# The second FFN in blocks of seven products, its LoRA added to the weights by an accumulating DMA

## What is computed

```
y  = x W^T + 2 * routed LoRA(x)                 # top 2 of 8 experts
x  = x + series(y) + FFN1(y)                    # six powers of a gate; FFN1 has 1248 hidden columns
z  = x W2^T + b + 2 * LoRA(x) of each sequence  # one of 32 adapters
h1 = z (w1 + 2 B1 A1)^T
h3 = z (w3 + 2 B3 A3)^T                         # FFN2 has 1376 hidden columns
g  = silu(h1) * h3
x  = x + g (w2 + 2 B2 A2)^T
```

## Time and profile before

| what | us |
|---|---|
| median of 3 runs | 448.58 (448.51 to 448.97) |
| the profiled execution itself | 448.42 |
| its span, first to last instruction | 446.7 |
| outside the span | 1.72 |
| PE busy | 441.4 of 446.7 |
| DVE busy | 324.0 |
| ACT busy | 212.2 |
| POOL busy | 29.3 |

### The profile page before, as it was taken

One profiled execution on the slowest core, in us unless ns is written; L12 is line 12 of the kernel. 1 busy time (PEld: TensorE's weight loads), 2 busy tenths in 40 slices (PEclk: granted clock), 3 DMA queues, 4 the chain that ended last, 5 costly groups with the idle time before them and its releaser, 6 DMA issues.

```text
span 446.7 us, 5568 instructions
## 1 busy us (share of the span) xinstructions
PE 441.4 (99%) x2009; PEld 363.5 (81%) x2009; DVE 324.0 (73%) x471; ACT 212.2 (48%) x324; POOL 29.3 (7%) x51
## 2 busy tenths in 40 slices
PE   8999999999999999999989999999999999999997
PEld 6788888888888888888778888888888888888886
DVE  5756699667989688896899248989853568887631
ACT  6364452345757447564565527365541124654300
POOL 1004100000001100005200000000000000000000
PEclk9999999999999999999999999999999999999999
DMA  8406800044574655657340010222201122121022
GB/s 301 132 0 195 201 0 1 12 119 117 117 190 118 147 133 121 145 138 198 109 150 6 18 48 18 70 66 61 74 2 41 57 91 66 48 66 53 1 102 87
DMA packets 20299, 40.44 MB, mean 91 GB/s; under 512 B 2672, under 2 KB 4736, under 8 KB 20272
## 3 DMA queue, kind: packets, MB, share of 16 engines
q1 hardware_dynamic: 16992, 32.51, 22.6%
q0 software_dynamic: 3280, 7.58, 9.7%
HBM read 37.98 MB, written 2.10 MB: 90 GB/s over the span
## 4 chain that ended last, share of the span: by engine, by line
PE 95%; DVE 3%; DMA 1%; ACT 0%; issue 0%; ACTq 0%
PE PS L1697 16%; PE PS L1698 16%; PE PS L1699 16%; PE PS L1562 15%; PE PS L1563 15%; PE PS L1564 15%; PE PS L1874 1%; DVE WU L938 1%; DMA X<-in_x 1%; DVE X L1180 1%; PE PS L1576 0%; PE PS L1922 0%; PE PS L1932 0%; PE PS L1933 0%; DVE S L1249 0%; DVE G L938 0%
## 5 line engine op out<-in xcount | busy, mean ns | idle before, releaser
L1697 PE MATMUL PS<-HT,WU 128*128 128x512 f32 x266 | 103.9, 391 | 1.3 <-DVE T L1123 1.0
L1698 PE MATMUL PS<-HT,WU 128*128 128x512 f32 x266 | 103.6, 389 | 0.0
L1699 PE MATMUL PS<-HT,WU 128*128 128x512 f32 x266 | 103.6, 389 | 0.0
L503 ACT ACTIVATE WU<-raw 128x256 fp32r<-128x256 f32 (+2 forms) x55 | 49.0, 897 | 31.0 <-PE PS L1699 15.1
L1697 PEld LDWEIGHTS PS<-HT,WU 128*128 128x128 f32 x266 | 50.0, 188 | 12.7 <-DVE T L1123 1.4
L938 DVE TENSOR_TENSOR WU<-raw,WU 128x256 fp32r<-128x256 f32 (+2 forms) x56 | 56.5, 1014 | 5.1 <-ACT WU L503 5.0
L1699 PEld LDWEIGHTS PS<-HT,WU 128*128 128x128 f32 x266 | 49.9, 188 | 10.5
L503 ACT ACTIVATE PS<-PS 128x512 f32<-128x512 f32 x46 | 26.8, 582 | 66.0 <-PE PS L1699 59.0
L1698 PEld LDWEIGHTS PS<-HT,WU 128*128 128x128 f32 x266 | 50.0, 188 | 10.0
L938 DVE TENSOR_TENSOR G<-T,G 128x1024 fp32r<-128x1024 f32 (+2 forms) x46 | 43.9, 967 | 12.2 <-ACT G L503 11.6
L503 ACT ACTIVATE G<-T 128x1024 fp32r<-128x1024 f32 (+2 forms) x47 | 39.8, 856 | 22.0 <-DVE T L1054 6.8
(11 more groups left out here) (170 smaller groups left out, 713.1 us busy)
## 6 DMA issues: line engine op xcount, KB each, us to landing
raw<-in_pieces SPq DMA_DIRECT2D x73, 256.0 KB, 3.0
raw<-in_parts SPq DMA_DIRECT2D x14, 512.0 KB, 3.6
raw<-in_parts POOLq DMA_DIRECT2D x14, 384.0 KB, 5.0
X<-in_x SPq DMA_DIRECT2D x8, 256.0 KB, 4.9
raw<-in_pieces SPq DMA_DIRECT2D x14, 128.0 KB, 2.8
out_x<-X SPq DMA_DIRECT2D x7, 256.0 KB, 2.0
su_raw<-in_stk_up POOLq DMA_DIRECT2D x6, 192.0 KB, 2.6
T<-in_lora_b POOLq DMA_DIRECT2D x16, 32.0 KB, 2.5
```

What stands on the lines that cost most here:

```text
L503: return nc.scalar.activation(o, i, ACT.Copy)
L1697: pe.matmul(bank, w[:, 1, cols], hi, start=start and kc == 0, stop=False, skip_group_check=not start)
L1698: pe.matmul(bank, w[:, 0, cols], low, start=False, stop=False, skip_group_check=not start)
L1699: mm = pe.matmul(bank, w[:, 0, cols], hi, start=False, stop=kc == 1, skip_group_check=not start)
```

## The change

The second FFN takes the form of the first. `BLOCKS` gets 13 blocks for it: up blocks for chunks 2 to 10 and four down blocks for chunks 2 to 9. Chunks 0 and 1 stay direct (four half steps of the down product for them in place of 12), and chunk 10 goes down directly at the very end, 3 matmuls for each output. From the third block of it on, the low-rank update goes another way: ScalarE copies it, times 2, from PSUM to a tile `delta` (`delta_hi`), GpSimd issues a DMA that adds `delta` to the raw weights in SBUF (`merge_by_dma`), and GpSimd computes the four weight sums itself (`sums`). `ga_raw` and small tiles move into the space of `delta`, which changes no order. At the end of the first FFN (`last`) VectorE does `add_d` ahead of `tail_lo(1)`, and one LoRA tile moves.

```diff
-LAST = len(BLOCKS) - 1
+
+BLOCKS = ([(0,) + b for b in [("u", 0), ("u", 1), ("u", 2), ("u", 3), ("u", 4), ("d", 0), ("d", 1),
+                              ("u", 5), ("u", 6), ("u", 7), ("u", 8), ("d", 2), ("d", 3), ("u", 9)]]
+          + [(1,) + b for b in [("u", 2), ("u", 3), ("u", 4), ("u", 5), ("u", 6), ("d", 0), ("d", 1),
+                                ("u", 7), ("u", 8), ("u", 9), ("u", 10), ("d", 2), ("d", 3)]])
+F2 = 14
+LAST, END = F2 - 1, len(BLOCKS) - 1
+TAIL = (8, 10)
...
+            def sums(q):
+                n = 3 * (merged_by_dma(q) - 1)
+                pool.wait_ge(merged_in, 16 * merged_by_dma(q))
+                pool.wait_ge(w_ready, max(P_TWO[q - 2], P_PASS + 1) + 1)
+                nc.gpsimd.tensor_tensor(sum_at(q, "S1"), raws(q, "A21"), raws(q, "A22"), ALU.add).then_inc(pool_step, 1)
+                nc.gpsimd.tensor_tensor(sum_at(q, "S3"), raws(q, "A11"), raws(q, "A21"), ALU.add).then_inc(pool_step, 1)
+                pool.wait_ge(pool_step, n + 1)
+                nc.gpsimd.tensor_tensor(sum_at(q, "S2"), sum_at(q, "S1"), raws(q, "A11"), ALU.add).then_inc(pool_step, 1)
+                pool.wait_ge(pool_step, n + 3)
+                nc.gpsimd.tensor_tensor(sum_at(q, "S4"), raws(q, "A12"), sum_at(q, "S2"), ALU.add).then_inc(sums_done, 1)
+
+            def merge_by_dma(q):
+                for p in (P_ONE[q], P_TWO[q]):
+                    pool.wait_ge(raw_in[SLOT[p]], raw_count(p))
+                pool.wait_ge(delta_out, merged_by_dma(q))
+                pool.dma_start(merge_region(q), delta[:], accum_op=ALU.add).then_inc(merged_in, 16)
+
+            for q in range(1, 4):
...
+            for q in range(F2 + 2, END + 1):
...
+                merge_by_dma(q)
+                sums(q)
...
+            def delta_hi(q):
+                n = merged_by_dma(q)
+                if n == 1:
+                    act.wait_ge(lora_ready, HALVES)
+                else:
+                    act.wait_ge(merged_in, 16 * (n - 1))
+                act.wait_ge(merge_done, MERGE["block", q] + 1)
+                nc.scalar.activation(delta[:], PS[:, 6:8, :].rearrange("p b n -> p (b n)"), ACT.Copy,
+                                     scale=SCALING).then_inc(delta_out, 1)
...
+                if q < END:
+                    part1_hi(q + 1, p4_done, q)
+                copy_bc(q)
+                if F2 < q <= END - 2:
+                    delta_hi(q + 2)
                 if odd:
...
                     x_out(q, "b")
...
+                if q == END - 1:
+                    merge_piece(P_END, 6)
+                if q == END:
+                    w_lo(P_END, tail_w(0))
+                    x_out(q, "c")
...
                 x_out(q - 1, "c")
-                s2_lo(1)
-                s2_lo(2)
-                add_b1(q)
+                for k in range(3):
+                    s2_lo(k)
+                add_b(q)
                 s2_lo(3)
                 tail_lo(0)
+                add_d(q)
                 tail_lo(1)
-                add_d1(q)
...
+            def block(q):
+                p6(q)
+                if F2 < q <= END - 2:
+                    merge_block(q + 2)
+                if q == END - 1:
+                    merge_piece(P_END, 10, slice(0, D), 6)
+                p5(q)
+                p2(q)
+                p7(q)
+                if q < END and q != LAST:
+                    p1(q + 1)
+                p3(q)
+                p4(q)
...
+            def merge_down(n, odd):
+
+                for j in range(4):
+                    bank = PB[6 + (1 - j % 2 if odd else j % 2)].rearrange("p (o j n) -> p j o n", o=2, j=2)[:, j // 2]
+                    o = S2_B + n % 2 * 2 * P
+                    mm = pe.matmul(bank, S2[:, chunk(2 + 4 * (n // 2) + j)], S2[:, o:o + 2 * P], start=True, stop=True)
                 mm.then_inc(merge_done, 1)
...
+                    (copied_e, END + 1), c_free(END), a_free(END), b_free(END), (out_ready, 1)]
+            for n, (h, o, cols, bank) in enumerate(OUTPUTS):
+                pe.wait_ge(*free[n])
+                pe.wait_ge(g_ready, G_SPLIT[1, 10, h])
+                product(PB[bank][:, cols], tail_w(0), tail_g(1, 10, h)[:, :, cols], chunk(o), True, True).then_inc(down2_done, 1)
```

More of the change, by code:

```diff
@@ L99 @@
 SLOT += [0, 1, 4, 5, 3, 2, 0, 1, 4, 5, 3]
[L100 to L110, removed]
+P_CLASSIC = len(SLOT)
+SLOT += [0, 1, 3, 2]
+for _q in range(F2, len(BLOCKS)):
+    if _q == F2 + 2:
+        P_PASS = len(SLOT)
+        SLOT += [4, 5]
+    P_ONE[_q], P_TWO[_q] = len(SLOT), len(SLOT) + 1
+    SLOT += ((0, 1), (3, 2))[_q % 2]
+P_END = len(SLOT)
+SLOT.append(3)
 PIECES = len(SLOT)
@@ L1479, in _ @@
             su_lo(2)
[L1480 to L1483 removed]
+            sums(F2 + 1)
+            part1_lo(F2 + 1)
+            add_b(F2)
+            add_d(F2)
             g_lo(1)
[L1485 to L1495 removed]
@@ L1553, in _ @@
+            add_b(F2 + 1)
+            add_d(F2 + 1)
+            for j in range(2):
+                w_lo(P_PASS + j, DW[:, j])
+            mul1(1, 3)
+            mul0(1, 3)
+            part1_lo(F2 + 2)
+            pass_add(0)
+            part2_lo(F2 + 2)
+            su_lo(3)
+            pass_add(1)
+            for q in range(F2 + 2, END + 1):
+                steady(q)
             for n, (h, c, cols, bank) in enumerate(OUTPUTS):
+                q = END - 1 if c < 2 else END
+                first = c % 2 == q % 2
+                dve.wait_ge(((out_c, out_a), (out_d, out_b))[h][first], outputs(q))
@@ L1908, in _ @@
+            p6(0)
+            p2(0)
+            p7(0)
+            p1(1)
+            p3(0)
+            p4(0)
+            for q in range(1, F2):
+                block(q)
             for h in range(HALVES):
-                for j in range(C1 - TAIL):
+                for j in range(C1 - TAIL[0]):
                     tail(h, j)
@@ new lines, in _ @@
+            p1(F2 + 1)
+            p3(F2)
+            p4(F2)
+            p6(F2 + 1)
+            for j in range(2):
+                merge_piece(P_PASS + j, j, slice(0, D), 6 + j)
+            p5(F2 + 1)
+            p2(F2 + 1)
+            p7(F2 + 1)
+            p3(F2 + 1)
+            p4(F2 + 1)
+            last = unit(1, 3) + 1
+            ready = [[(copied_e, F2 + 2), (silu[0], last - 1), (silu[1], last - 1), (g_mul[0], last)],
+                     [(pass_added, 1), (silu[0], last), (silu[1], last), (pass_added, 4)]]
@@ new lines, in _ @@
+            for n in range(4):
+                if n == 1:
+                    merge_block(F2 + 3)
+                if n == 3:
+                    p1(F2 + 2)
+                half_step(n, ready[n // 2])
+            for q in range(F2 + 2, END + 1):
+                block(q)
+            pe.wait_ge(w_ready, P_END + 1)
+            free = [a_free(END - 1), b_free(END - 1), (merged, MERGED["piece", P_END]), (delta_out, merged_by_dma(END)),
+                    (copied_e, END + 1), c_free(END), a_free(END), b_free(END), (out_ready, 1)]
@@ L2055, in ffn, with block_pieces @@
         return up_piece, down
+    def block_pieces(up_piece, down, q):
+        _, what, c = BLOCKS[q]
+        if what == "u":
+            return [up_piece(c, k, q % 2) for k in range(2)]
+        first = 4 * (c // 2) + 2 * BLOCKS[q][0]
+        rows = [[first + k, first + 2 + k] for k in range(2)]
+        return [np.concatenate([down[j][:, o * P:(o + 1) * P] for o in (2 * (c % 2), 2 * (c % 2) + 1)
+                                for j in rows[k]], axis=1) for k in range(2)]
     def first_ffn():
```

1162 lines of the change are left out of this document (463 added, 699 removed).

## The result

The changed kernel takes **449.57 us** (median of 20 runs, 448.69 to 450.63), the kernel before 448.89 (20 runs beside it, 448.44 to 449.34): ratio 1.0018, interval 1.0012 to 1.0024. It is slower by 0.18%, where 444.8 was forecast. The profiled run of after is the slowest of its 20, 450.63 us; that of before took 448.42.

A forecast was written before the change was run, and what follows sets the result against it. PE (TensorE) was taken as the bound, busy 441.4 of 446.7 us. 448.42 - 5.57 - 0.6 + 1.7 + 0.25 = 444.2, plus 0.5 is 444.7; with the median 0.16 above the profiled run, 444.8 us, range 443.2 to 449.0.

The forecast's parts named there:

- What leaves PE: Matmuls dropped from PE, 14 of 512 columns and 20 of 256, save 5.57 us.
- The reading of the waits: Before the change PE has three waits only: 1.1 us at the start, 1.0 and 0.3 ending the first FFN.
- The end of the first FFN: One tail split moves behind `add_d` of the last block; PE's wait falls from 1.0 to 0.4, saving 0.6 us.
- The last piece: In the last block PE waits 1.7 us for VectorE's split of piece `P_END`; bounds 0.5 and 2.3.
- The round through ScalarE, the DMA and GpSimd: Second FFN's weight merge and sums: transfer 5.9 us, additions 0.7 each, sums ready with 4.4 us of room.
- Rival 2: GpSimd's serial round outlasts the 10.0 us block, from 0.95 us an addition on; 451 us at 1.2; chance 0.14.
- the 0.5 us for "a GpSimd that works on the same memory": Allowance of 0.5 us (0 to 4) for the four blocks after an odd chunk, where VectorE has 1.5 us room.
- Rival 1: GpSimd's additions and VectorE's sums and splits take turns after odd chunks; 2.8 us more, 447.1; chance 0.18.
- the outputs, taken at 0: At the kernel's end additions and writes keep up with products 0.68 us apart; cost 0, bounds 0 and 0.7 us.
- Where the forms meet: Second block of the second FFN: `add_b` needed at 5.9, done at 6.1; 0.25 us lost (0 to 1.0).
- Rival 3: More than forecast: last-block VectorE work covered, or no contention and no meeting loss; 443.2 to 444.0 us; chance 0.10.

The follow-up runs named there:

- ninth kernel: On the eighth kernel, PE makes the first two last products between `p3` and `p4` of the last block, one split of `g` precedes `add_d`: 444.90 us, ratio 0.9916.
- kernel 11: The kernel after with `tail_lo(1)` back ahead of `add_d` at the end of the first FFN, as before the change: 450.23 us, ratio 1.0031.
- Kernel 5: The kernel after with the split of the last piece ahead of `add_d`, on both ScalarE and VectorE: 448.18 us, ratio 0.9980.
- kernels 3 and 4: The kernel after with GpSimd's four additions cut to one column (447.44 us, 0.9956), or replaced by four fills of 1024 columns that read nothing (447.28 us, 0.9964).
- kernel 1: The kernel after run again unchanged, as a base: 449.53 us, ratio 1.0012.
- Kernel 2: The kernel after with the weight sums back on VectorE, merges still by ScalarE and the DMA: 446.81 us, ratio 0.9949.
- Kernel 10: The eighth kernel with half of the columns of six output writes left out, all arithmetic kept: 444.86 us, ratio 0.9914.
- eighth kernel: The kernel after with three mends: sums on VectorE, last piece's split early, SU splits early: 445.53 us, ratio 0.9918.
- kernel 6: The kernel after with the SU splits moved from the block's end to right behind part 2, on ScalarE and VectorE: 448.66 us, ratio 0.9990.
- kernel 7: The kernel after with merges and sums of the weights on VectorE as before, so the block form alone: 448.79 us, ratio 0.9995.

## Why the prediction was wrong

**What leaves PE** (5.57 us): right. The records fell by 34, and the ninth kernel shows that they are worth time: with the waits taken away it is 3.9 us under before, and 1.15 of small losses and 0.75 of a longer end are still in it. The reading of the waits left out one of 0.3 us at the very start (PE for VectorE's G, at 5.14); nothing hangs on it.

**The end of the first FFN** (0.6): right; the wait fell from 1.0 to 0.4, and kernel 11 gives the 0.6 back.

**The last piece** (1.7): right as a wait, 1.93 as lost time. Kernel 5 removes it. The whole of it isn't won by that, since the outputs behind it then queue.

**The round through ScalarE, the DMA and GpSimd**: it fits, as forecast. The transfers from `delta` land after 4.5 us where 5.9 was taken from the row of the same kind; the additions take 0.73 alone where 0.7 was chosen between 0.37 and 1.22 (0.56 by the estimate from the Trainium skill, "GPSIMD Engine Reference", 3.1 Elementwise); GpSimd waits for ScalarE's `delta`, 16.1 us in seven of eleven places. ScalarE waits for GpSimd once, 3.0 us at 314.95, and PE loses nothing there. **Rival 2 is false.** It was nearer than that sounds: beside VectorE the four additions take 4.3 us, 1.08 each, over the 0.95 from which the sum had rival 2 decide, and only the quicker landing made up for it. But all this room was for GpSimd, and GpSimd was not what came last.

**The step that failed first: the 0.5 us for "a GpSimd that works on the same memory".** Rival 1 named the mechanism, at a chance of 0.18 and 2.8 us; kernels 3 and 4 show that the reading of the additions is what does it. In place of 0.5 us it cost 2.5 of PE's time (5.7 lost in kernel 1, 3.2 and 3.1 in kernels 3 and 4), or 2.1 to 2.4 of the measured time. I held it unlikely because the additions start before the block begins, so that only some of them would meet VectorE's splits. The trace shows that most do: 29 of the 44 took longer than alone, in the rounds that made PE wait three of four. VectorE is busy nearly all the time in a block after an odd chunk, and an addition that has waited through a 1.75 us split ends 1.5 us later and meets the next instruction also. Chance comes in at one point, who starts first: that moves the 0.76 us near 335 between two profiles of one program. Kernel 2 gives back 2.7, which looks like rival 1's 2.8, but that is luck in part: 2.1 of it are PE's, and the other 0.7 lie at the end, which kernels 3 and 4 leave as it was. So those 0.7 do not come from GpSimd's reading.

**The step that failed second: the outputs, taken at 0**; they cost 1.5 us. The working had all numbers: 0.69 us for a write, 0.68 for a product, 0.60 for an addition. It compared rates and found that each keeps up. But where the rates leave nothing over, each delay on the way stands at the end in full. In the kernel after the third addition starts 0.35 late; the additions make that good at 0.60 against 0.68, the writes at 0.69 can't, and are a good 0.9 us behind at the end: 445.60 (last addition) + 0.9 (the time from the first addition's end, 440.79, to the first bytes, at 441.69) + 0.3 (128 KB) would have the last bytes out at 446.8, and they go until 447.7. The additions themselves end 0.79 after PE in place of 0.46. That makes 1.2 of the 1.5 us. Kernel 10 shows, in the eighth kernel, 0.5 to hang on the amount of bytes.

The late start of the third addition goes with half of it. Kernels 1, 3, 4, 6 and 11 have it too (0.35 to 0.37 us), and their ends are 4.0 to 4.1 us long; kernels 2 and 7, which have the same nine outputs in the same order, do not, and theirs are 3.4 and 3.5. In the traces that have it, the DMA engines also carry an 8 KB piece of the program's own instructions, which starts 0.7 to 1.1 us after the late addition and among the first writes (at 442.98 in after); kernels 2 and 7 have none of that size there. Kernel 5, where the additions queue without a pause, has one as well and ends after 4.5 us. That the two belong together is seen, that one makes the other is not shown.

**Overlooked: the LoRA tile SU**, 1.0 us. It stands last in VectorE's list of the block, and the merge that needs it comes early in the next one. No term of the prediction had it. It is the place where VectorE's lateness shows and no loss of its own: kernel 6 removes it by another place in the list, but kernels 2, 3 and 4, which leave SU where it is, lose 0.01 us there. It is a part of the 2.5 us above. In kernel 7 it is there (0.97) without any work of GpSimd's, in a kernel where VectorE has the merges and the sums.

**Where the forms meet**: 0.44 for 0.25; the mechanism is right.

So rival 1 was true, at 447.1 by its own sum. The end, which had no price, adds 1.5, and the last piece and the meeting place 0.4 over their terms: 449.0 of the 449.57. The remaining 0.6 is not taken apart. **Rival 3** is false.

What stays open: why the third of the last additions is 0.35 us late (the profile names no one for it), and how exactly the end's 1.5 us divide, since kernel 10 was made on the eighth kernel, where VectorE is late at the outputs, and not on the kernel after.

## What to carry to other kernels

Additions given to GpSimd are free only if VectorE doesn't read two SBUF operands meanwhile; ask of VectorE's instructions there how many SBUF inputs they have, and if VectorE is busy without a break, count most additions as meetings (here 29 of 44). When work moves, list each consumer of the relieved and the loaded engine that comes last in its list (here SU and the last piece) and ask what it costs if that engine is late. At the end of a kernel compare starts as well as rates: products, additions and writes that each take 0.6 to 0.7 us in step have nothing to catch up with.

The best kernel keeps the block form, the merge through ScalarE and the DMA, leaves the sums on VectorE, and moves three splits and two outputs: 0.9916 of before.

## What the runs showed of the hardware

- An accumulating DMA within SBUF (512 KB) lands 4.5 us after its issue, and 5.3 at most, beside 5.0 for 384 KB that come from HBM by the same kind of transfer in the same trace.
- GpSimd adds 256 float columns in 0.73 us alone, 2.2 to 2.3 us beside a split of 1536 columns by VectorE, and fills 1024 in 0.96. Its additions of one column still took 0.27 to 0.68 on the mean.
- While GpSimd fills, VectorE's instructions with two SBUF inputs keep their length (1748 ns against 1751 before); while it adds, the same one takes 2.32 us in the worst place, if the addition started first, and 1.75 if the split did.
- Output writes of 256 KB, one behind another, go at 372 to 385 GB/s, 0.69 us each.
